# Layer-norm preparation of the first graph layer: own semaphores for the row loads, statistics one group ahead, first adjacency tile transposed in between

## The reference

```python
h = jnp.maximum(_layernorm(x, axis=-1), 0.0)
x = x + _L0_gnn_ref(h, adj, L0_gnn_weight, L0_gnn_bias)
...
def _layernorm(x, axis=-1, eps=1e-05):
    m = jnp.mean(x, axis=axis, keepdims=True)
    v = jnp.var(x, axis=axis, keepdims=True)
    return (x - m) / jnp.sqrt(v + eps)
...
h = input @ weight                              # first layer
out = jnp.maximum(adj @ h + bias, 0.0)
return _graph_pool(out, adj)                    # maximum over neighbours
```

## Time and profile before

| | us |
|---|---|
| median of 3 executions | 1737.51 (1735.72 to 1738.18) |
| the profiled execution, its own time | 1733.34 |
| its span, first to last instruction | 1731.3 |
| busy: TensorE matmul, VectorE | 1557.3, 1276.2 |
| busy: ScalarE, GpSimd | 700.7, 571.4 |

### The profile page before, as it was taken

One profiled execution on the slowest core, in us unless ns is written; L12 is line 12 of the kernel. 1 busy time (PEld: TensorE's weight loads), 2 busy tenths in 40 slices (PEclk: granted clock), 3 DMA queues, 4 the chain that ended last, 5 costly groups with the idle time before them and its releaser, 6 DMA issues.

```text
span 1731.3 us, 37002 instructions
## 1 busy us (share of the span) xinstructions
PE 1557.3 (90%) x11433; PEld 1025.4 (59%) x11433; DVE 1276.2 (74%) x3508; ACT 700.7 (40%) x1113; POOL 571.4 (33%) x792
## 2 busy tenths in 40 slices
PE   3699999978889888899998999699999999988996
PEld 3467767756677676666655666578644444445553
DVE  5499999988899999635665677532399999983454
ACT  2434444425555555123342323466556555540000
POOL 2423222337777777201110000133200000017776
PEclk9999999988999999999999999899999999999998
DMA  4477777743343333222213322244200000005553
GB/s 159 163 269 272 287 263 294 278 170 91 105 121 104 112 102 114 83 97 93 89 61 97 97 85 88 77 121 128 85 1 7 6 6 6 6 19 166 168 163 86
DMA packets 97579, 205.12 MB, mean 118 GB/s; under 512 B 10912, under 2 KB 61728, under 8 KB 89328
## 3 DMA queue, kind: packets, MB, share of 16 engines
q1 hardware_dynamic: 73008, 172.58, 29.0%
q0 software_dynamic: 11840, 25.52, 5.3%
q10 hardware_dynamic: 12672, 6.29, 1.2%
HBM read 178.13 MB, written 26.21 MB: 118 GB/s over the span
## 4 chain that ended last, share of the span: by engine, by line
PE 49%; DVE 22%; issue 15%; POOL 7%; DMA 3%; ACT 2%; DVEq 1%; POOLq 1%; SPq 1%; ACTq 0%
PE bank L688 17%; PE bank L557 7%; PE bank L756 6%; DVE partsA L2085 6%; POOL gath L1391 4%; PE bank L642 4%; PE bank L823 4%; PE bank L562 2%; PE bank L542 2%; DVE gath L1681 2%; DVE cand L1548 2%; PE bank L522 2%; DMA gath<-last_features,IDX 2%; PE bank L586 1%; PE bank L512 1%
## 5 line engine op out<-in xcount | busy, mean ns | idle before, releaser
L688 PE MATMUL bank<-partsB,panel 128*128 128x387 bf16 (+1 forms) x2048 | 350.3, 332 | 16.5 <-POOL partsB L1181 8.7
L688 PEld LDWEIGHTS bank<-partsB,panel 128*128 128x128 fp8e4 x2048 | 201.8, 99 | 160.8 <-issue 12.7
L823 PE MATMUL bank<-wide,partsA 128*128 128x512 f32 x512 | 263.2, 596 | 6.4 <-ACT rows L1105 4.9
L642 PE MATMUL bank<-partsB,first 128*128 128x128 bf16 x3072 | 222.9, 222 | 38.0 <-DVE gath L1681 21.6
L1548 DVE MAX8 cand<-bank 128x8 f32<-128x128 f32 x1024 | 216.7, 279 | 39.4 <-POOL found L1214 19.9
L642 PEld LDWEIGHTS bank<-partsB,first 128*128 128x128 fp8e4 x3072 | 195.4, 99 | 83.0 <-issue 64.8
L557 PE MATMUL bank<-partsA,panel 128*128 128x387 bf16 x1024 | 216.5, 334 | 22.6 <-DVE cand L1548 15.1
L890 ACT ACTIVATE panel<-bank 128x1024 fp8e4<-128x1024 bf16 x128 | 130.7, 1023 | 172.9 <-PE bank L542 172.9
L1303 POOL DMA_INDIRECT gath<-pool_features,idx_now x160 | 162.8, 1017 | 55.2 <-issue 46.6
L1105 ACT COPY rows<-bank 128x512 f32<-128x512 f32 x256 | 133.3, 615 | 116.3 <-DVE partsA L2101 87.6
L1681 DVE TENSOR_REDUCE gath<-bank 128x128 f32<-128x512 f32 x256 | 173.1, 681 | 8.6 <-PE bank L642 8.1
(11 more groups left out here) (274 smaller groups left out, 2099.6 us busy)
## 6 DMA issues: line engine op xcount, KB each, us to landing
rows<-in_adj SPq DMA_DIRECT2D x64, 1024.0 KB, 7.2
panel<-adjT_panels SPq DMA_DIRECT2D x128, 512.0 KB
adjT_panels<-panel SPq DMA_DIRECT2D x32, 512.0 KB, 3.0
panel<-adjT_panels SPq DMA_DIRECT2D x64, 256.0 KB, 2.9
gath<-pool_features,idx_now POOLq DMA_INDIRECT x160
overflow_maxima<-wide POOLq DMA_DIRECT2D x1, 2048.0 KB, 17.4
pool_features<-gsc ACTq DMA_DIRECT2D x8, 256.0 KB, 2.3
rows<-overflow_maxima SPq DMA_DIRECT2D x8, 256.0 KB
```

The source lines that it names most:

```text
L642: i = pe.matmul(first_bank(n, peeled)[:, b * P:(b + 1) * P], first[:, q % 2, j, :], pparts[:, j, k * FE:k * FE + F], start=(k == 0), stop= ...
L688: i = pe.matmul(bank[q][:, 0:3 * w], panel[:, q, j, :], of_block if w < FE else parts_of[u][:, j, :], start=(j == 0), stop=(j == NT - 1))
L823: pe.matmul(o[:, :], zs[:, q % 2, :], zT[:, c * 512:(c + 1) * 512], start=True, stop=False)
```

## The change

The row loads after the first group are split in two (tiles 4 to 11, tiles 12 to 31), each with its own semaphore; the other eight loads are waited for later, by VectorE and TensorE when the preparation is done. The copy to `xg` goes away: statistics and normalising read `X` in place. VectorE takes the statistics of group g + 1 before it normalises group g; mean, variance and root have two buffers each for it, borrowed from tensors that are free at that time. In groups 2 to 5 TensorE transposes one step of adjacency tile 0 between the turning and the product, and ScalarE takes it out after its part 0; the peeled first tile of the main loop falls away. TensorE's wait for the last `gsc` moves into the fourth chunk of the first product. The loops over groups on TensorE, ScalarE and VectorE are written out.

```diff
         D2INV = sb("D2INV", [P, NT], F32)
         own_code = D2INV
+        first_mv = [mv, d2[:, :, 0:nc.vector.BN_AGGR_DIM]]
+        first_std = [std, v[0]]
         sg = sb("sg", [P, G, TOP], F32)
...
         s_loaded = sem("inputs_loaded")
         s_first_rows = sem("first_rows_loaded")
+        s_more_rows = [sem(f"other_rows_loaded{i}") for i in range(2)]
         s_w0 = sem("first_weights_loaded")
...
             xr = x.rearrange("(t p) f -> p t f", p=P)
             sp.dma_start(X[:, 0:G, :], xr[:, 0:G, :]).then_inc(s_first_rows, 16)
             sp.dma_start(W["W0"][:, :], w0).then_inc(s_w0, 16)
-            sp.dma_start(X[:, G:NT, :], xr[:, G:NT, :]).then_inc(s_loaded, 16)
+            sp.dma_start(X[:, G:3 * G, :], xr[:, G:3 * G, :]).then_inc(s_more_rows[0], 16)
+            sp.dma_start(X[:, 3 * G:NT, :], xr[:, 3 * G:NT, :]).then_inc(s_more_rows[1], 16)
             for t, a in loads:
                 sp.dma_start(t[:, :], a).then_inc(s_loaded, 16)
             for k, a in (("b0", b0), ("b31", b31), ("b32", b32)):
...
                                       start=True, stop=True)
                 i.then_inc(s_hw, 1)
-            def aux0(g, peeled):
-                aux_transposes(0, g)
-                aux_products(0, g)
-            turns(pe, aux0)
-            pe.wait_ge(s_loaded, 16 * 9)
             def transposes(g, q, c):
                 if c % 2 == 0:
...
                     i = pe.transpose(o[:, b * P:(b + 1) * P], rb[:, j * P:(j + 1) * P, 1], identb[:, :])
                 i.then_inc(s_tr, 1)
+            for g in range(NG):
+                aux_transposes(0, g)
+                if 2 <= g < 6:
+                    transposes(0, 0, g - 2)
+                aux_products(0, g)
+            pe.wait_ge(s_loaded, 16 * 8)
             def product_chunk(g, q, c, wait_parts):
                 t = g * G + q
                 if wait_parts:
                     pe.wait_ge(s_parts, c + 1)
+                    if c == 3:
+                        pe.wait_ge(s_gsc, NG + 1)
                 if c == 0:
                     pe.wait_ge(s_agg, t + 1)
                 pe.wait_ge(s_panel, 4 * t + c // 2 + 3)
...
                 i.then_inc(s_code, 1)
             def turn(g, peeled):
-                for q in range(G):
+                for q in range(1 if peeled else 0, G):
                     before = (g, q - 1) if q else (g - 1, G - 1)
                     for c in range(NT // BPB):
                         if c % 2 == 0:
                             transposes(g, q, c // 2)
-                        if not (peeled and q == 0):
-                            product_chunk(*before, c, peeled and q == 1)
+                        product_chunk(*before, c, peeled and q == 1)
             turns(pe, turn)
             for c in range(NT // BPB):
                 product_chunk(NG - 1, G - 1, c, False)
...
                 part0(u, g)
                 part1(u, g)
-            def turn(g, peeled, second=False):
-                std_of(0, g)
+            def first_std_of(g):
+                act.wait_ge(s_mv, g + 1)
+                if g > 1:
+                    act.wait_ge(s_rstd, g - 1)
+                act.activation(first_std[g % 2][:, :], first_mv[g % 2][:, :, 1], ACT.Sqrt, bias=eps_ln[:, 0:1]
+                               ).then_inc(s_std, 1)
+            def evac_chunk(t, q, c):
+                act.wait_ge(s_tr, 4 * t + c + 1)
+                act.sem_inc(waited["act"], 1)
+                act.activation(panel[:, q, c * 8:(c + 1) * 8, :].rearrange("p b i -> p (b i)"),
+                               bank[2 + c % 2][:, :].bitcast(BF16), ACT.Copy, saturate=False
+                               ).then_inc(s_panel, 1)
+            first_std_of(0)
+            for g in range(NG):
+                if g + 1 < NG:
+                    first_std_of(g + 1)
                 hT_of(0, g)
-                if not (peeled or second):
+                if g > 1:
                     part1(0, g - 2)
-                if not peeled:
+                if g > 0:
                     part0(0, g - 1)
-            turn(0, True)
-            turn(1, False, True)
-            with act.Fori(2, NG) as g:
-                turn(g, False)
+                if 2 <= g < 6:
+                    evac_chunk(0, 0, g - 2)
             part1(0, NG - 2)
             split(0, NG - 1)
...
                     act.wait_ge(s_stored[q], 16 * g)
                     act.wait_ge(s_code, 8 * (t - G + 1))
                 for c in range(4):
-                    act.wait_ge(s_tr, 4 * t + c + 1)
-                    act.sem_inc(waited["act"], 1)
-                    act.activation(panel[:, q, c * 8:(c + 1) * 8, :].rearrange("p b i -> p (b i)"),
-                                   bank[2 + c % 2][:, :].bitcast(BF16), ACT.Copy, saturate=False
-                                   ).then_inc(s_panel, 1)
+                    evac_chunk(t, q, c)
             def feat_store(g):
                 act.wait_ge(s_post, 2 * (g + 1))
...
             def turn(g, peeled):
                 for q in range(G):
-                    evac_panel(g, q, peeled)
+                    if not (peeled and q == 0):
+                        evac_panel(g, q, peeled)
                     if q == 1 and not peeled:
                         feat_store(g - 1)
                         part0(1, g - 1)
...
             pool.wait_ge(s_blank, 32)
             pool.wait_ge(s_feat, 16 * NG)
-            pool.wait_ge(s_loaded, 16 * 9)
+            pool.wait_ge(s_loaded, 16 * 8)
             pool.wait_ge(s_flag, 1)
             def after_chunk(t, c):
...
             dve.wait_ge(s_const, 8)
             dve.wait_ge(s_first_rows, 16)
             for s, k in ((s_gsc, 1), (s_agg, 2), (s_sum, 4), (s_code_used, 4), (s_fp_used, 4), (s_gath_used, 2), (s_over_clear, 1),
-                         (s_keyused, 2), (s_gen_used, 1)):
+                         (s_keyused, 2), (s_gen_used, 1), (s_x, NG)):
                 dve.sem_inc(s, k)
...
                     dve.tensor_copy(gsc[:, :, 0:F], ps).then_inc(s_gsc, 1)
-            def turn(g, peeled):
-                if not peeled:
-                    dve.wait_ge(s_loaded, 16 * 9)
+            def first_stats(g):
+                if g > 0:
+                    dve.wait_ge(s_mv, g)
+                if g == 1:
+                    dve.wait_ge(s_more_rows[0], 16)
+                if g == 3:
+                    dve.wait_ge(s_more_rows[1], 16)
+                for q in range(G):
+                    i = dve.bn_stats(st[:, q, :], X[:, g * G + q, :])
+                i.then_inc(s_stats, 1)
+                dve.wait_ge(s_stats, g + 1)
+                if g > 1:
+                    dve.wait_ge(s_norm, g - 1)
+                dve.sem_inc(waited["dve"], 1)
+                for q in range(G):
+                    i = dve.bn_aggr(first_mv[g % 2][:, q, :], st[:, q, :])
+                i.then_inc(s_mv, 1)
+            def first_norm(g):
+                dve.wait_ge(s_std, g + 1)
+                if g > 0:
                     dve.wait_ge(s_norm, g)
+                dve.reciprocal(rstd[:, :], first_std[g % 2][:, :]).then_inc(s_rstd, 1)
+                dve.wait_ge(s_rstd, g + 1)
+                if g > 0:
                     dve.wait_ge(s_hTp, g)
-                dve.tensor_copy(xg[:, :, :], grp(X, g)).then_inc(s_x, 1)
-                normalise(0, g)
-                if not peeled:
+                dve.sem_inc(waited["dve"], 1)
+                for q in range(G):
+                    i = dve.tensor_scalar(hn[:, q, :], X[:, g * G + q, :], first_mv[g % 2][:, q, 0:1], rstd[:, q:q + 1],
+                                          ALU.subtract, ALU.mult)
+                i.then_inc(s_norm, 1)
+            first_stats(0)
+            for g in range(NG):
+                if g + 1 < NG:
+                    first_stats(g + 1)
+                first_norm(g)
+                if g > 0:
                     operand(0, g - 1)
-            turns(dve, turn)
             operand(0, NG - 1)
+            dve.wait_ge(s_loaded, 16 * 8)
             def take_product(u, T, q):
```

## The result

| | before | after |
|---|---|---|
| median of 4 executions, us | 1737.14 (1735.72 to 1738.18) | 1756.90 (1754.33 to 1759.31) |
| profiled execution, its span | 1733.34, 1731.3 | 1754.33, 1752.6 |
| first product of the adjacency | 66.73 | 46.10 |
| VectorE's restart behind the blank rows | 88.11 | 74.06 |

The ratio after to before is 1.0113 (95% interval 1.0097 to 1.013): 1.1% or some 20 us slower, where 1725.5 was predicted. The restart comes 14.05 us earlier, two more than predicted, and the end comes 21.3 us later. So about 35 us are lost behind the part of the program that the change rewrites.

A forecast was written before the change was run, and what follows sets the result against it. VectorE's restart at 88.11, waiting for the blank rows to land, was taken as the bound. Preparation 8.0 us plus landing 4.1 made 12.1 us: median 1725.5, forecast gain 10 to 14 us (0.45), 8 in 10 from 1718 to 1732.5.

The forecast's parts named there:

- Behind it: Main loop after VectorE's restart: tile 2 already loaded, tile 3 landing with the blank rows, the rest costed at nothing.
- shifted by the same 12 us: Sign for the forecast: after VectorE's restart at 76, everything up to the end comes 12 us earlier.
- Bound at the blank rows' landing: First tile: VectorE stands still 9.2 us until 88.11 because GpSimd's `found` waits 15.9 us for the blank-row store.
- Loads, T(0), T(1): Start of the preparation: with split row loads, the turnings of groups 0 and 1 on TensorE start at 10.0 and 13.9.
- The round: Preparation from group 3, one turning to the next: 5.5 us, then 5.4 each, against 5.8; last turning 8.0 us earlier.
- rival A: Preparation: GpSimd's work slides off the normalising, rounds 4.3 to 4.4 us, last turning at 40.2; gain 16 to 22 us; chance 0.2.
- the bound of 42: Sign of being wrong: group 7's turning, the last on TensorE, starting before 42 us (or after 48.5); forecast 45.3.
- Tile 0's transposes and evacuations at nothing: Preparation: adjacency transposes on TensorE and four ScalarE evacuations of 1.02 us each cost nothing while the rows are there.
- its rows in group 2: Sign of being wrong: TensorE waiting for adjacency rows there; first half tile expected at 18.8, needed at 19.4.
- From T(7) to the store: GpSimd's unchanged queue from the start of group 7's turning to the first blank-row store: 15.5 us, store issued at 60.8.
- Blank rows, 4.1 us less: Blank-row store, issue to landing: 14.3 us instead of 18.6, as tile 2 and panel 0 move earlier; bounds 0 and 9.
- Rival D, the granted clock: TensorE idles longer and the lower clock lasts 30 us more after the restart: slower, 1741; chance 0.03.

## Why the prediction was wrong

The direction was wrong, and one step made it so: the paragraph **"Behind it"**, with "I cost the rest at nothing", and the sentence that everything after the restart would be shifted by the same 12 us. It asked what VectorE, TensorE and the rows would do in the main loop, and left out that the edit changes the length of VectorE's own code ahead of that loop. Written-out loops were listed as part of the change and given no price. The missing term measures +35.0 us. The sum with it: 14.05 us earlier at the restart, 35.0 later from the waits, 21 us slower; the spans differ by 21.3. The same change with its code rolled up, and so without the waits, is 33.6 us faster by the medians (1723.26 against 1756.90). Even there the shift at the restart isn't the shift at the end: of 15.5 us 12.9 are left.

The other steps, in their order:

- **Bound at the blank rows' landing**: right. It still ends VectorE's idling, and when it is taken away 8.0 to 12.9 us go with it.
- **Loads, T(0), T(1)**: 10.01 and 13.65 against 10.0 and 13.9.
- **The round**: too long. From T(2) to T(7) the changed kernel takes 23.1 us, 4.6 a round, where I had 5.4 to 5.5 and rival A 4.4. The last turning at 41.05 was below the bound of 42 that I had set for "wrong", and nearer to rival A's 40.2 than to my 45.3. GpSimd's two instructions are not locked to VectorE's round in one phase. Rounds of 5.0 to 5.4 and of 3.2 occur in one execution, and I took the worst phase for all. The Trainium skill's rule of the exclusive port (SBUF — State Buffer, section on the two separate sides) agrees with the single instruction (up to 1.25 us instead of 0.34). What it makes of a round depends on the phase, which neither my round nor rival B's took in.
- **Tile 0's transposes and evacuations at nothing**: right. With them left out of the rounds the last turning starts at 40.77 instead of 41.05. TensorE did wait for its rows in group 2, which I had named as a sign of being wrong, but for 0.61 us only, until 19.69.
- **From T(7) to the store**: 15.4 us against 15.5.
- **Blank rows, 4.1 us less**: 1.8 less by issue and landing (56.47 to 57.62 + 15.7 = 73.3, so 16.85 us, against 18.6). I had divided bytes by a rate, as if the store were served evenly with the row loads; the time doesn't bear that out, and in what order the transfers were served was not looked at. With the round's error of 4.3 us the other way, 14.05 instead of 12.1. (My own terms also differ by 0.2: 60.8 + 14.3 is 75.1, not 75.3.)
- **Rival D, the granted clock**: not the cause. The clock is lower in the windows with the stalls (0.91 from 200 to 240 us, against 1.00 before), but TensorE idles there, waiting for VectorE, and the waits alone close the sum to 0.4 us. No rival of mine held the cause, and the chance of 0.03 for slower covered only the clock.

## What to carry to other kernels

When an edit lengthens or shortens the code of an engine ahead of a long loop on that engine, count the instructions, and then look at two rows: the instruction queue's packets in a window inside the loop, and waits for "issue" at the jump back. A loop that fits without fetching shows none of either; moving it by a few instructions, or rolling up what stands ahead, is enough to get there. And a wait belongs in front of the first instruction that needs it: the one for the blank rows could stand three tiles later, and moving it was worth 8.0 us in the kernel before, and in the rolled one as much as the whole new preparation (12.9 us).

## What the runs showed of the hardware

- A backward jump of VectorE can stop it for about 7 us (at the longest 6.8 to 8.3 in four kernels), five jumps costing 35 to 42 us of waits, while the same 272 instructions elsewhere jump in 0.4 us. It depends on the position of the loop, and comes back after 128 instructions (moved by 105, 113 and 233: bad; by 0, 60, 88, 95, 125, 145: good). Why a miss takes as long as 7 us with four or five packets a turn stays open.
- The instruction queue that changes with VectorE's code, q14, moves packets of 8 KB; the other one, q8, packets of 16 KB (31 packets, 0.51 MB, in both kernels).
- The granted clock is lower where a stall stops TensorE: from 176 to 184 us it was 0.86, against 1.00 in the kernel before.
- The same kernel took 1736 us on two chips and 1912 to 1935 on a third, at a granted clock of 0.93 instead of 0.97. The difference arises behind the first 360 us.
